# Moving eight row scatters by two groups inside the first attention unit

## What is computed

```python
    Q = x @ W_Q.T ; K = x @ W_K.T ; V = x @ W_V.T          # 16 heads of 32
    attn = jnp.einsum('bhqd,bhkd->bhqk', Q, K) * scale      # causal mask, softmax
    y = jnp.einsum('bhqk,bhkd->bhqd', probs, V)
    x = _layernorm(x + y @ W_O.T, axis=-1)
    weights, top1 = max and argmax of softmax(x @ router_w.T + router_b)
    y = (x @ expert_w[top1].T + expert_b[top1]) * weights
    x = _layernorm(x + y, axis=-1)
```

## Time and profile before

| | us |
|---|---|
| median of 3 runs | 2460.68 |
| lowest, highest | 2455.18, 2462.23 |
| the profiled execution | 2472.75 |
| its span, first to last instruction | 2471.0 |
| mean granted TensorE clock in it | 0.989 of full speed |
| PE, DVE, ACT, POOL busy | 94%, 59%, 42%, 35% of the span |

### The profile page before, as it was taken

The page is one execution under the profiler, slowest core; times in us unless marked ns, Lnnn a source line. Parts: engine busy times, 40 slices in busy tenths (PEclk is TensorE's granted clock), DMA queues, the critical chain, the costliest instruction groups (busy, mean ns, idle before and its releaser), DMA issues.

```text
span 2471.0 us, 41896 instructions
## 1 busy us (share of the span) xinstructions
PE 2313.1 (94%) x14080; PEld 1480.6 (60%) x14081; DVE 1457.8 (59%) x3929; ACT 1026.2 (42%) x2112; POOL 865.8 (35%) x1525
## 2 busy tenths in 40 slices
PE   1999999999999999999999999999999999949998
PEld 1754575547654775467555755476546754538887
DVE  2577366745765376646673566547753677466665
ACT  2245524452346334542455244623453245533333
POOL 2332324232433332333333242324233331336665
PEclk9999999999999999999999999999999999969999
DMA  8533145323532253215431354135331534234443
GB/s 294 147 99 97 63 120 144 103 69 86 158 100 95 71 161 99 78 65 146 120 112 60 98 151 121 65 85 155 95 108 45 155 91 138 74 113 147 154 149 120
DMA packets 131298, 281.07 MB, mean 114 GB/s; under 512 B 33096, under 2 KB 42320, under 8 KB 128818
## 3 DMA queue, kind: packets, MB, share of 16 engines
q1 hardware_dynamic: 102114, 210.76, 28.9%
q0 software_dynamic: 27472, 67.49, 9.2%
q10 hardware_dynamic: 1536, 0.53, 0.1%
HBM read 133.04 MB, written 46.48 MB: 73 GB/s over the span
## 4 chain that ended last, share of the span: by engine, by line
PE 80%; DVE 6%; SPq 5%; ACT 3%; DMA 2%; issue 2%; POOL 1%; POOLq 0%; ACTq 0%; DVEq 0%
PE y_ps L1359 12%; PE proj L1270 10%; PE den_ps L1359 10%; PE score L1339 10%; PE maxp L1327 8%; PE proj L1382 5%; PE proj L1283 5%; SPq L519 4%; PE maxp L1523 4%; PE score L1523 4%; PE proj L1327 3%; PE maxp L1339 2%; ACT probs L890 2%; PE score L1382 2%; DVE tile_max L1014 2%
## 5 line engine op out<-in xcount | busy, mean ns | idle before, releaser
L890 ACT ACTIVATE probs<-score 128x512 f32<-128x512 f32 (+3 forms) x1216 | 562.8, 493 | 551.3 <-PE score L1339 523.1
L726 POOL TENSOR_SCALAR_AFFINE_SELECT probs<-probs 128x256 f32<-128x256 f32 x512 | 217.1, 428 | 712.4 <-ACT probs L890 709.5
L1019 DVE CUSTOM_DVE_ANT_0 maxp<-maxp,mask_qk 128x384 f32<-128x384 f32 (+3 forms) x696 | 323.5, 506 | 219.6 <-PE maxp L1327 191.1
L1339 PE MATMUL score<-q_stack,k_stack 97*128 97x512 f32 (+2 forms) x1216 | 426.3, 373 | 26.4 <-ACT probs L890 24.3
L1270 PE MATMUL proj<-xt,w_qk 128*128 128x512 f32 x1284 | 364.0, 400 | 54.5 <-DMA w_qk<-w_qk_parts 53.7
L1327 PE MATMUL maxp<-k_stack,q_stack 96*128 96x512 f32 (+2 forms) x1024 | 329.6, 365 | 14.7 <-DVE tile_max L1014 4.4
L1359 PE MATMUL y_ps<-probs,v 128*32 128x512 f32 (+3 forms) x3072 | 327.7, 498 | 12.1 <-DVE rows L1044 12.0
L1359 PE MATMUL den_ps<-probs,ones_f 128*32 128x512 f32 (+3 forms) x3072 | 319.3, 486 | 0.0
L1339 PEld LDWEIGHTS score<-q_stack,k_stack 97*128 97x128 f32 x1216 | 224.5, 189 | 142.8 <-ACT probs L890 96.0
L1270 PEld LDWEIGHTS proj<-xt,w_qk 128*128 128x128 f32 x1284 | 238.3, 191 | 110.7 <-DMA w_qk<-w_qk_parts 51.1
L1327 PEld LDWEIGHTS maxp<-k_stack,q_stack 96*128 96x128 f32 x1024 | 180.6, 189 | 140.8 <-DVE tile_max L1019 47.5
(11 more groups left out here) (164 smaller groups left out, 3166.6 us busy)
## 6 DMA issues: line engine op xcount, KB each, us to landing
w_qk<-w_qk_parts SPq DMA_DIRECT2D x64, 512.0 KB
q_stack<-w_vo_parts SPq DMA_DIRECT2D x16, 2048.0 KB, 8.2
q_stack<-parts SPq DMA_DIRECT2D x512, 64.0 KB
k_stack<-parts SPq DMA_DIRECT2D x512, 64.0 KB
rows<-dispatched SPq DMA_DIRECT2D x75, 257.0 KB
xt_raw<-x_t SPq DMA_DIRECT2D x32, 512.0 KB, 3.7
q_stack<-parts POOLq DMA_DIRECT2D x256, 64.0 KB, 2.3
k_stack<-parts POOLq DMA_DIRECT2D x256, 64.0 KB, 2.4
```

The lines of the kernel that those rows point to most:

```text
L726: nc.gpsimd.affine_select(out=block, in_=block, compare_op=ALU.is_ge, fill=0.0, base=0, pattern=[[0, 2], [1, P]], channel_multiplier=-1)\
L890: nc.scalar.activation(probs[:, 4 * (n % PROBS) + h, c:BANK], score_bank(u, 4 * j + h)[:, c:BANK], ACT.Exp, scale=SCALE).then_inc(exp_done ...
L1019: top = nc.vector.tensor_tensor_reduce(out=tile, in0=tile, in1=mask_qk[:, BANK - cols:BANK], scale=1.0, scalar=-3.0e38, op0=ALU.add, op1=A ...
L1339: nc.tensor.matmul(score_bank(u, i)[:, c0:BANK], k_st[u % SETS][0:3 * DH + 1, h, kb * P:(kb + 1) * P], q_st[u % SETS][0:3 * DH + 1, h, t * ...
```

## The change

The eight scatters of the batch before stand in the groups 2 to 5 of unit 0, two in each, where they stood in the groups 0 to 3. Nothing else is different.

```diff
-        SCATTER_AT = {0: (0, 1), 1: (2, 3), 2: (4, 5), 3: (6, 7)}
+        SCATTER_AT = {2: (0, 1), 3: (2, 3), 4: (4, 5), 5: (6, 7)}
```

## The result

The changed kernel takes 2503.65 us (median of 4 runs, 2498.23 to 2510.02) where the kernel before takes 2458.0 us beside it: a ratio of 1.0179, 95% interval 1.0150 to 1.0208, or 44 us more (37 to 51). The prediction was 2493 us with a range of 2474 to 2508. The direction and the mechanism were right; the size forecast was 32 us where 44 were measured.

A forecast was written before the change was run, and what follows sets the result against it. PE, running in program order, was taken to bound the kernel. Seven stalls of 3.4 us (24 us) plus 8 us of lowered clock, less 0 of gain, made 32 us on the median 2460.7: 2493 us, range 2474 to 2508.

The forecast's parts named there:

- The mechanism: Unit 0, group 6: DVE's copy waits for the last scatter, PE's weighing of group 4 for the copy, in seven batches.
- When the last scatter is issued: POOL in unit 0: the last scatter's issue ends at 665.5 in the third batch, 7.1 us later than before.
- Landing: Time for a scatter to land before DVE's copy in group 6: 2.9 us, bounds 2.1 and 4.1.
- From the copy to PE: Unit 0: PE's weighing of group 4 starts 0.83 us after DVE's copy starts.
- The stall: PE before the weighing of group 4: 3.4 us late in each of seven batches, 24 us, between 18 and 32.
- a price of scatters among the groups 0 to 3: Unit 0, first mask to weighing of group 3: scatters cost 0.8 us a batch; gain taken as 0, at most 5 us.
- The clock: PE's clock falls behind most of the seven stalls: 1.2 us each on average, 8 us in all, bounds 0 and 11.
- The backed-up queue: Rival: the last scatters land in 6 us, each stall costs 8 to 9 us, about 2520 us; chance 9%.
- The stall without the clock's fall: Rival: PE stalls before group 4's weighing but the clock stays at 1.00, +24, 2485 us; chance 22%.
- Not slower: Rival: scatters land before DVE wants the copy in group 6, up to 5 us faster, 2455 us; chance 3%.
- Half of the stall regained: Rival: PE's later waits in units 0 and 1 shrink, no clock loss, +12, 2473 us; chance 9%.

The follow-up runs named there:

- the divided kernel: The changed kernel with the wait split over two semaphores, so the first half's copy waits only for the first four scatters: 2458.22 us, ratio 0.9996.
- the kernel with the shorter stalls: The changed kernel with 8 extra matmuls on PE in front of group 4's weighing in the seven batches with scatters: 2494.33 us, ratio 1.0138.
- the kernel with the last pair in front of the send: The changed kernel with the last two scatters in group 4 before the second send, not in group 5 behind it: 2472.43 us, ratio 1.0046.

## Why the prediction came out as it did

**The mechanism** held at each point that it named: a DVE idle time before L1044 in group 6, ended by the scatters' DMA; a PE idle time before the weighing, ended by DVE's rows; seven times and not in the first batch; a clock below 1.00 behind it.

**When the last scatter is issued**: predicted 665.5 - 641.8 = 23.7 us behind the first mask, measured 23.6 in two batches and 24.0 to 24.5 in the other five, 24.1 on the mean. In those five the first scatter started 0.94 us behind its mask, with "issue" as the reason, in place of 0.17. It was not the wait for the destinations: DVE had finished them (L1005) over 9 us before. What held the issue was not tried.

**Landing**: 2.9 us taken from the nearest row, measured 2.68 to 2.96 from the end of the issue to the copy, 2.83 on the mean. That the two agree is luck. The view behind rows 5 counts from the start of the issuing instruction, and the prediction added its 2.9 us to the end of one. An issue of the expert stage takes 1.08 us by itself:

```profile
L784 POOL DMA_INDIRECT out<-rows,dest x72: 969/1075/1128, 2225.0 to 2466.7; - x72
```

From the end of the issue the nearest row says 1.8 us, and these scatters took 1.0 us longer; a sum from 1.8 us would have given a stall of 2.3 us in place of 3.4. The Trainium skill, "DMA: Bandwidth & Descriptors", section "Anatomy of one DMA — SWDGE (gpsimd) path", gave an estimate of 2.6 us. Counted from the end of the issue it was a little short of the 2.83 us measured, counted from its start, from which 3.8 us were measured, it was 1.2 us short; the measurement decides.

**From the copy to PE**: 0.83 us, measured 0.84.

**The stall, 3.4 us predicted, 4.6 measured.** This is the first mis-sized term. 0.4 us of it are the later issue. 0.8 us are the point from which the lateness was counted: the copy stood at 23.0 us in the execution read and stands at 22.2 in the others. The prediction saw this difference, 19.38 against 18.61 us, took it for a price of scatters among the groups 0 to 3, and set it to zero with a possible gain. Two other executions with the scatters in these groups don't show it, so it is no price that this placing must pay. It made the room in front of the copy look 0.8 us larger than it was. The expected gain in the divided kernel (0.998) failed for the same reason.

**The clock, 1.2 us predicted, 2.15 measured.** The second mis-sized term. The one fall in rows 11 and 12 came at a time when PE was already busy again, and cost 1.5 us. Behind the stalls of 3.9 to 4.7 us the clock fell in all seven batches of both executions, each time while PE was still idle, and in the third batch it stayed low from 671.3 to 678.2. PE worked from 672.98 on, so 5.2 us of its work ran at half the clock; that gives an estimate of 2.6 us lost, and 8.20 - 5.80 = 2.4 us are measured. In the kernel with the shorter stalls the four falls came only after PE had started again, and cost 1.6 us each. The fall from which the prediction took its price had less of PE's work under it, some 3 us by rows 12, which fits its lower cost. At this stall falls were also more frequent the longer PE was idle; that the length alone decides is not shown, and the falls behind 1.4 to 2.2 us at other places speak against it.

The corrected sum, 7 x (4.6 + 2.15) = 47 us, is 3 to 5 us above the measured 42 to 44. That is inside the first interval and at the upper end of the second. Whether a little of the stall is regained later stays open: from the weighing of group 5 to the next batch's first mask the two executions of the changed kernel take 234.96 and 233.43 us on the mean and the two of the kernel before 234.47 and 234.60, so executions of one kernel differ by more than is looked for.

**The rivals.** The backed-up queue did not come: the scatters landed in under 3 us. The stall without the clock's fall did not come either: the clock fell behind fourteen of fourteen stalls; it is what the kernel with the last pair in front of the send shows. Not slower: refuted, as the last issue ended 24.1 - 22.2 = 1.9 us behind the moment at which the copy was wanted. Half of the stall regained: not borne out, as only 3 to 5 of the 47 us are missing in the measured times.

No kernel here beats the one before by more than the measurement can tell. The divided wait makes the place of the scatters free, 0.9996 with the late places, and gives nothing by itself.

## What to carry to other kernels

A DMA issue that is moved on a queue with time to spare is not free if somebody counts its landing. Compute the deadline from the consumer's side: the moment at which the waiting engine wants its go, less the landing time (and see from which point a view counts it), less everything that stands on the issuing queue in front of the last DMA counted; here one group later cost nothing and two groups 44 us. Where a consumer needs only some of the DMAs, a semaphore for each part removes the deadline. Before a difference between two batches of one trace is priced as a mechanism, look whether a second execution shows it.

## What the runs showed of the hardware

A stall of PE was paid for twice here, as idle time and as clock. At the stall in group 6, with idle times of 1.4 to 2.4 us, the clock stayed at its upper level of 2.4 GHz in seven of seven cases; with 1.9 to 2.8 us it fell to 1.2 GHz in four of seven, at 1.6 us each; with 3.9 to 4.7 us it fell in fourteen of fourteen, at some 2.15 us each. The length of the idle time alone does not tell whether it falls: at other places it fell behind 1.40 us in the kernel before and behind 1.46, 1.53, 1.84 and 2.18 us in the kernel with the last pair in front of the send, and it stayed up behind others of 1.5 and 1.6 us. Extra matmuls with no use, 16 of 0.24 us in each stall, made the kernel 13 to 15 us faster (1.0111 for 1.0171 on one chip).

Indirect scatters of 257 KB, issued by GpSimd while the DMA engines were busy for some 0.86 of the time, landed 2.2 to 3.5 us after the end of their issue, in one case 4.3 (counted up to the copy that waited for them).
